# Moving a layer norm into a recurrence, and four buffers instead of two for one weight stream

## The reference, cut to what matters

```python
h = layernorm(x) * (1 + ca) + sa
x = x + ga * gated_linear_attention(h)      # 4 heads, DK 1024, DV 2048, recurrence over tokens
h = layernorm(x) * (1 + cb) + sb
x = x + gb * moe(h)                         # 8 experts, top-2 gates; computed densely:
# for e in range(8): out += gate[:, e:e+1] * (gelu(h @ w1[:, e, :]) @ w2[e])   # 1024 -> 2048 -> 1024
```

## Time and profile before

| | us |
|---|---|
| median of three executions | 3591.79 |
| lowest | 3590.21 |
| the profiled execution | 3595.84 |
| its span, slowest core (core 0) | 3594.3 |
| its span, fastest core (core 2) | 3559.4 |

### The profile page before, as it was taken

How to read it: one execution, slowest core, us unless ns; L and a number is a source line. 1 busy time by engine, 2 the same in 40 slices (tenths; PEclk the granted TensorE clock), 3 DMA queues, 4 the chain that set the end, 5 groups by cost and what they waited for, 6 DMA issues and landing times.

```text
span 3594.3 us, 37009 instructions; the slowest of 8 cores (3559.4 to 3594.3 us)
## 1 busy us (share of the span) xinstructions
PE 2705.0 (75%) x12923; PEld 1259.1 (35%) x12923; DVE 927.4 (26%) x1769; ACT 804.7 (22%) x1456; POOL 266.4 (7%) x463
## 2 busy tenths in 40 slices
PE   1474566457646855369999999999279999999997
PEld 0152235124412522124444444444034444444443
DVE  0323242332233333521122212211522112221221
ACT  0314232422342143220121112101321112111210
POOL 0000001001001100000000000000000000000000
PEclk9785678578757866689999999999689999999998
DMA  9451235034303611123434343434024444444444
GB/s 209 67 98 21 36 61 91 1 47 78 64 0 47 111 30 26 19 47 59 83 59 83 63 78 61 80 61 80 1 47 71 71 76 71 71 71 72 72 77 137
DMA packets 84362, 233.49 MB, mean 65 GB/s; under 512 B 7851, under 2 KB 8236, under 8 KB 82006
## 3 DMA queue, kind: packets, MB, share of 16 engines
q0 software_dynamic: 82400, 214.09, 35.9%
q1 hardware_dynamic: 1782, 17.03, 1.3%
HBM read 436.76 MB, written 8.39 MB: 124 GB/s over the span
## 4 chain that ended last, share of the span: by engine, by line
PE 65%; DVE 9%; ACT 9%; DMA 9%; issue 6%; DVEq 0%; ACTq 0%; POOL 0%; POOLq 0%
PE p L787 23%; PE p L808 23%; PE p L547 7%; PE p L672 4%; PE p L467 3%; DMA bigbuf<-wmod 3%; DVE S L656 2%; ACT S_bf L660 2%; DMA wvg<-w2t 2%; DMA vslab<-w1t 2%; DMA ogbuf<-WgTt 1%; ACT bigbuf L603 1%; ACT scratch L626 1%; DMA ogbuf<-WvTt 1%; ACT scratch L618 1%
## 5 line engine op out<-in xcount | busy, mean ns | idle before, releaser
L808 PE MATMUL p<-bigbuf,wvg 128*128 128x512 bf16 x4096 | 902.7, 383 | 44.6 <-DVE bigbuf L798 35.5
L787 PE MATMUL p<-hbuf,vslab 128*128 128x512 bf16 x4096 | 903.3, 383 | 18.2 <-ACT bigbuf L794 9.7
L794 ACT ACTIVATE bigbuf<-p 128x512 bf16<-128x512 f32 x512 | 305.7, 597 | 1467.0 <-PE p L787 1428.4
L808 PEld LDWEIGHTS p<-bigbuf,wvg 128*128 128x128 bf16 x4096 | 402.4, 99 | 544.9 <-issue 77.8
L787 PEld LDWEIGHTS p<-hbuf,vslab 128*128 128x128 bf16 x4096 | 402.0, 98 | 515.9 <-issue 51.4
L817 DVE SCALAR_TENSOR_TENSOR xTsb<-p,modc,xTsb 128x512 f32<-128x512 f32 x256 | 180.4, 746 | 756.1 <-PE p L808 756.1
L798 DVE TENSOR_TENSOR bigbuf<-bigbuf,vslab 128x1024 bf16<-128x1024 bf16 x256 | 177.2, 692 | 762.5 <-ACT bigbuf L794 762.5
L547 PE MATMUL p<-ogbuf,hbuf 128*128 128x256 bf16 x1024 | 153.3, 323 | 103.3 <-DMA ogbuf<-WgTt 52.4
L777 POOL DMA_DIRECT2D vslab<-w1t x128 | 90.3, 707 | 1079.9 <-PE p L787 994.4
L547 PEld LDWEIGHTS p<-ogbuf,hbuf 128*128 128x128 bf16 x1024 | 117.2, 116 | 137.0 <-issue 107.6
L402 POOL DMA_DIRECT2D wvg<-w2t x128 | 68.3, 535 | 878.2 <-PE p L808 817.2
(11 more groups left out here) (130 smaller groups left out, 1573.4 us busy)
## 6 DMA issues: line engine op xcount, KB each, us to landing
vslab<-w1t POOLq DMA_DIRECT2D x128, 512.0 KB, 5.9
wvg<-w2t POOLq DMA_DIRECT2D x128, 512.0 KB, 5.2
hbuf<-WoutTt POOLq DMA_DIRECT2D x51, 256.0 KB, 5.1
bigbuf<-wmod POOLq DMA_DIRECT2D x8, 1536.0 KB, 16.7
wvg<-WvTt POOLq DMA_DIRECT2D x16, 512.0 KB, 9.1
ogbuf<-WvTt POOLq DMA_DIRECT2D x16, 512.0 KB, 5.1
wvg<-WgTt POOLq DMA_DIRECT2D x16, 512.0 KB, 8.6
ogbuf<-WgTt POOLq DMA_DIRECT2D x16, 512.0 KB, 5.2
```

Of the source, the lines that this page charges most:

```text
L787: T(lambda e, k=k, n2=n2, mi=mi, wb=wb, pbk=pbk: e.matmul(pbk[:, :], wb[:, mi * 1024 + k * 128: mi * 1024 + (k + 1) * 128], hbuf[:, k * 10 ...
L794: C(lambda e, m=m, n2=n2, pbk=pbk: e.activation(out=bigbuf[:, m * 1024 + n2 * 512: m * 1024 + (n2 + 1) * 512], in_=pbk[:, :], func=AF.Gelu ...
L808: T(lambda e, k=k, n2=n2, wb=wb, pbk=pbk: e.matmul(pbk[:, :], wb[:, k * 128:(k + 1) * 128], bigbuf[:, k * 1024 + n2 * 512: k * 1024 + n2 * ...
```

## The change

- `ln_slab` takes the two PSUM banks that it works in as arguments, p0 and p1 unless told otherwise, where it had p2 and p3.
- The norm of slab 0 is emitted ahead of the slab loop. That of slab `s + 1` is emitted inside slab `s`, ahead of the recurrence's block `t4 = 1`.
- L412 and L415 now *write* `bv` beside their staging tile.
- In each expert pass the w2 stream gets four buffers, two of them in `gslab[:, 4096:8192]`. The w1 stream keeps its two.

```diff
-        def ln_slab(s, scale_off, bias_off, dst_c0, dst_stride):
+        def ln_slab(s, scale_off, bias_off, dst_c0, dst_stride, pA=None, pAb=None,
+                    pB=None, pBb=None):
+            if pA is None:
+                pA, pAb, pB, pBb = p0, pb["p0"], p1, pb["p1"]
...
-                    reads=[bxT[s], bv], writes=[bxbf_s[sl2]])
+                    reads=[bxT[s]], writes=[bxbf_s[sl2], bv])
...
-                    reads=[bxT[s], bv], writes=[bx2bf_s[sl2]])
-                T(lambda e, d=d, sl2=sl2: e.matmul(p2[0:1, :], ones_col, xbf_s[sl2],
+                    reads=[bxT[s]], writes=[bx2bf_s[sl2], bv])
+                T(lambda e, d=d, sl2=sl2: e.matmul(pA[0:1, :], ones_col, xbf_s[sl2],
...
+        ln_slab(0, 8, 0, 0, 512)
         for s in range(NSLAB):
             c0 = s * SLAB
-            ln_slab(s, 8, 0, 0, 512)
             for k in range(8):
...
             for t4 in range(4):
+                if t4 == 1 and s + 1 < NSLAB:
+                    ln_slab(s + 1, 8, 0, 0, 512)
                 tau = s * 4 + t4
...
+                wvg_pool[0] = [wvg[:, 0:2048], wvg[:, 2048:4096],
+                               gslab[:, 4096:6144], gslab[:, 6144:8192]]
+                bwvg_pool[0] = [bwvg[0], bwvg[1], buf("w2x0"), buf("w2x1")]
                 for md in range(8):
                     wb, wbb = stream_wvg_chunk(w2_d[e_i], md, 16, 128)
```

More of the change, by code:

```diff
@@ L417, in ln_slab @@
                     func=AF.Square),
-                    reads=[bxT[s], bv], writes=[bx2bf_s[sl2]])
-                T(lambda e, d=d, sl2=sl2: e.matmul(p2[0:1, :], ones_col, xbf_s[sl2],
+                    reads=[bxT[s]], writes=[bx2bf_s[sl2], bv])
+                T(lambda e, d=d, sl2=sl2: e.matmul(pA[0:1, :], ones_col, xbf_s[sl2],
                                                    start=(d == 0), stop=(d == 7)),
-                  reads=[bxbf_s[sl2], buf("consb")], writes=[pb["p2"]])
-                T(lambda e, d=d, sl2=sl2: e.matmul(p3[0:1, :], ones_col, x2bf_s[sl2],
+                  reads=[bxbf_s[sl2], buf("consb")], writes=[pAb])
+                T(lambda e, d=d, sl2=sl2: e.matmul(pB[0:1, :], ones_col, x2bf_s[sl2],
                                                    start=(d == 0), stop=(d == 7)),
-                  reads=[bx2bf_s[sl2], buf("consb")], writes=[pb["p3"]])
-            V(lambda e: e.tensor_single_scalar(out=rowsA, in_=p2[0:1, :],
+                  reads=[bx2bf_s[sl2], buf("consb")], writes=[pBb])
+            V(lambda e: e.tensor_single_scalar(out=rowsA, in_=pA[0:1, :],
                                                scalar=1.0 / D, op=ALU.mult),
-              reads=[pb["p2"]], writes=[brA])
+              reads=[pAb], writes=[brA])
             V(lambda e: e.tensor_tensor(out=rowsB[0:1, :], in0=rowsA, in1=rowsA,
@@ L430, in ln_slab @@
               reads=[brA], writes=[brB])
-            V(lambda e: e.scalar_tensor_tensor(out=rowsB[0:1, :], in0=p3[0:1, :],
+            V(lambda e: e.scalar_tensor_tensor(out=rowsB[0:1, :], in0=pB[0:1, :],
                                                scalar=1.0 / D, in1=rowsB[0:1, :],
                                                op0=ALU.mult, op1=ALU.subtract),
-              reads=[pb["p3"], brB], writes=[brB])
+              reads=[pBb, brB], writes=[brB])
             C(lambda e: e.activation(out=rowsB[0:1, :], in_=rowsB[0:1, :], func=AF.Sqrt,
@@ L439, in ln_slab @@
               reads=[brB], writes=[brB])
[L440 to L443, removed]
+            T(lambda e: e.matmul(pA[:, :], onesrf[0:1, :], rowsA, start=True, stop=True),
+              reads=[buf("onesrf"), brA], writes=[pAb])
+            T(lambda e: e.matmul(pB[:, :], onesrf[0:1, :], rowsB[0:1, :], start=True, stop=True),
+              reads=[buf("onesrf"), brB], writes=[pBb])
             for d in range(8):
@@ L448, in ln_slab @@
                 V(lambda e, d=d, c0=c0, scr_s=scr_s: e.scalar_tensor_tensor(
-                    out=scr_s, in0=p2[:, :], scalar=-1.0,
+                    out=scr_s, in0=pA[:, :], scalar=-1.0,
                     in1=xT[:, d * N + c0: d * N + c0 + SLAB], op0=ALU.mult, op1=ALU.add),
-                    reads=[pb["p2"], bxT[s]], writes=[bsc_s])
+                    reads=[pAb, bxT[s]], writes=[bsc_s])
                 V(lambda e, d=d, scr_s=scr_s: e.tensor_tensor(
-                    out=scr_s, in0=scr_s, in1=p3[:, :], op=ALU.mult),
-                    reads=[bsc_s, pb["p3"]], writes=[bsc_s])
+                    out=scr_s, in0=scr_s, in1=pB[:, :], op=ALU.mult),
+                    reads=[bsc_s, pBb], writes=[bsc_s])
                 C(lambda e, d=d, dst_c0=dst_c0, dst_stride=dst_stride, scr_s=scr_s: e.activation(
```

## The result

| | before | after |
|---|---|---|
| median of all executions beside one another (16 each), us | 3607.85 | 3629.51 |
| lowest | 3586.05 | 3618.48 |
| the profiled execution | 3595.84 | 3631.91 |
| its span, slowest core | 3594.3 (core 0) | 3630.4 (core 1) |
| its span, fastest core | 3559.4 | 3582.5 |

Ratio 1.0085, 95% interval 1.0064 to 1.0106: the changed kernel is slower by 0.64 to 1.06%, some 30 us where 22 were forecast. In a part of all executions a die runs at a lower clock whatever the kernel; the medians contain such executions, the ratios leave them out.

A forecast was written before the change was run, and what follows sets the result against it. It took a full TensorE to bound the expert passes and an engine-to-engine chain the attention. Terms +12.6 + 21.4 - 6 - 6 = +22.0 us on 3595.84 gave 3617.8, as a median 3614 us; range 3594 to 3638.

The forecast's parts named there:

- What bounds: Expert passes: TensorE full; attention recurrence: a chain hopping between engines, none full; slab norm: PE waits 11.67 us at its end.
- part 1: Heads of slabs 1 to 3: with the norm gone, L477 starts 0.14 us behind L677, removing 25.4 us each.
- Part 2: Recurrence: the moved norm stands in the chain because engine queues run in order, so the move hides nothing.
- Part 3: Norms: writing `bv` serialises casts and squares at 1.26 us a pair; move +12.6 us net, other five norms +21.4.
- the forecast's upper bound: Chain in the norms: handovers of 0.14 us instead of 0.10, 0.6 us more for each of eight norms, some 5 in all.
- the recurrence term: Recurrences of slabs 0 to 2: the norm with its chain of casts and squares adds 29.6 us a slab.
- Part 4: Slab heads: L477 follows dense matmuls at full clock, gaining 2 us a slab, -6 us in all.
- Part 5: Expert passes: four w2 buffers remove PE's waits for w2 transfers, -6 us, and the stall isn't passed on.
- The rival of the slower side: Expert passes: deeper w2 stream delays w1's last chunk, up to 7 us a pass, 112 in all, 3732; chance 0.05.
- The sum: Whole kernel: +12.6 + 21.4 - 6 - 6 = +22.0 us, median 3614, +0.6%, read as no change; chance 0.82.

The follow-up runs named there:

- e2_move: Kernel before with only the norms moved into the recurrence, staging tiles guarded once, casts and squares not writing `bv`, two w2 buffers: ratio 1.0005.
- e6_spread: Kernel after without the `bv` writes, staging tiles in `wvg`, the next slab's norm cut up over the recurrence's sixteen head steps and behind: ratio 0.9742.
- e9_nochain: Kernel after without the chain: casts and squares don't write `bv`, staging tiles guarded once as in e2_move; ratio 0.9987 to the kernel before.
- e1_chain: Kernel before with one edit, L412 and L415 write `bv`; norms at their old place, two w2 buffers: ratio 1.0130.
- e5_slots: e1_chain with eight pairs of staging tiles instead of two in the attention's norms: 3628.53 us in a single execution, no ratio.
- e3_w2: Kernel before with four w2 buffers and nothing else: ratio 1.0008.
- e10_w1only: Kernel before with four w1 buffers (two more in `ogbuf`) and nothing else: ratio 0.9991 (0.9956 to 1.0026).
- e7_w1deep: Kernel after with four w1 buffers, two more in `ogbuf`: ratio 0.9962 to the kernel before.
- e11_w1w2: Kernel before with four w1 and four w2 buffers: ratio 0.9903, from two executions.

## Why the prediction was off

Step by step, against its own terms:

- **What bounds, and part 1.** Right. The gap behind Wout shrank by 25.8 us (25.4 forecast); L480 follows L682 by 0.15 us (0.14).
- **Part 2, nothing is hidden.** Right, and tested by e2_move: +27.0 us for a norm without the chain, with it 30.7 (29.6 forecast). What the Trainium skill (TensorE: Matmul & The Clock Gate, "Architectural detail: the array is 16× 32×32, not 1× 128×128") says of the strict order of ACT and DVE holds in this trace: DVE's L599 starts at 354.48, behind the norm's last L455. e6_spread shows the other side: the idle time can be used by whoever places the instructions in it.
- **Part 3, the chain.** Right in kind, too small in size; this is the first step that failed. "That is 1.26 us a pair" counted two handovers of 0.10 us, taken from L624 and L660, which have one wait instruction each. From the third on, a cast has three, with the one that holds it up in front, and starts 0.24 us behind the square. The first two casts have fresh tiles, so six pairs of a norm are dearer by 0.13, 0.8 us a norm; the forecast's upper bound gave each handover 0.04 more, 0.6 a norm. The expert part's norms grew by 21.0 us where 16.6 were forecast (2 x (4.8 + 3.5)), of which the dearer pairs are 3; the recurrence term came out 1.1 a slab higher, of which they are 0.8. The rest of the 4.4 and 1.1 isn't traced to an operation.
- **Part 4, the clock.** Right: 1.89 us for L480 (1.9), projections of slabs 1 to 3 shorter by 1.7 each (2), 5.1 us in all (6).
- **Part 5, four w2 buffers.** Right on the mean core (-8.1, 6 forecast), wrong for the kernel; this is the second step that failed. "A stall that goes here isn't passed on" looked at one core. The w2 waits went on all cores, and on the trailing core of each pair longer waits for w1 took their place (13.7 to 18.3 us, and 2.7 to 6.5 on the leading ones). The time is that of the slowest core, a trailing one, whose passes were 1894 us before (mean of cores 0, 3, 4 and 6) and are 1893 after (cores 1, 3, 5 and 7), while those of the leading ones fell from 1884 to 1868. The term was worth 0. The rival of the slower side had a deeper w2 stream hurting w1, but within one core, at 112 us; the harm is there on the trailing core of a pair alone, and is about as large as its gain.
- **The sum.** Forecast +22.0. With the chain at its measured size (14.7 instead of 12.6 for the move, 21.0 instead of 16.6 for the expert part) it is +28.5, with nothing for w2 +34.5; measured is +0.85%, +30.5 on 3590, between 23 and 38. The profiled executions differ by 36.1. The range, 3594 to 3638, holds what 0.85% makes of 3592, 3622; it does so by a margin that was meant for something else, an overlap inside the recurrence, and that is luck.
- **How it was read.** This is the third step that failed: "A measurement of this kernel can tell about 2% (72 us) from no change, so this is no change." With sixteen executions of each the interval is 0.4% wide, so a loss of 0.6% could be told, and the change showed as a slowdown of 0.64 to 1.06%. "No change" was the wrong word for a sum of +22.0 with its own bounds at +15 and +39.

The cause of the slowdown is shown by taking it away (e9_nochain) and by adding it alone (e1_chain). The 0.24 us of the cast are shown by its wait instructions in the trace and by e5_slots. That the neighbour's burst is what delays a w1 chunk isn't shown as directly: it rests on the coincidence in time, which would fit other leading cores' bursts too, on the order of the spans by pairs, on e3_w2's and e10_w1only's one-sided waits, and on the pair's coming together in e7_w1deep and e11_w1w2. No run moved one core's bursts alone.

## What to carry to other kernels

A dependency that is declared for safety is paid for like real work: count for each operation all that it waits for, also what is fulfilled already, put the wait that will end last behind the others (argued from the trace, not run), and guard a tile once instead of tying its users to each other. Moving a block of instructions into another stage's idle time gains nothing while it stays in one piece in an in-order queue; cut to one piece a step it was hidden almost wholly. Where several cores stream at once, judge a buffer by the slowest core in several executions, and look for names that cover two buffers: here the stage with one such name became some 34 us a slab shorter without it, nearly a third of it by the clock that no longer fell in the waits.

## What the runs showed of the hardware

- The two cores of a pair go apart where weights are streamed: in every kernel with a shallow stream one core of each pair was 17 to 32 us behind the other, in changing roles, and with both streams deep 5 to 9 us. In all 11 executions of the kernel after the four slowest cores were one of each pair.
- Each engine that an operation waits for cost a wait instruction of its own in the queue, 0.07 us apart: a cast on DVE started 0.10 us behind ACT with one, and 0.24 with three of which the first was the last to be fulfilled (46 of 46 on core 1 of the kernel after). From DVE to ACT it took 0.08 with three, where the late one stood last.
- Two chunks of w2 (64 matmuls) took 1.69 us longer when the granted clock was at 0.50 for a part of them, behind the same 2.22 us of waiting; what core 1 lost in its passes beyond its waits for weights, 34 us, was more than these waits, 18.3.
- Sixteen expert passes with no wait for a transfer take 1854 us on every core. The kernel before took 1877 to 1902, of which its waits for transfers were only 7 to 17.
- 512 matmuls of the v and gate projections kept PE busy for 66 us at a granted clock of 0.85 and for 56 us at 1.00, where no wait for a transfer stood between them.
